# Row-column attention layer on one core: Yh kept in two f16 parts from the first half on, batch norm moved behind the product

## The reference

```
k = softmax over all 4096 pixels;  context = k v^T;  content_out = context^T q
Sx[n,i,x,y] = sum_d q[n,d,x,y] Px[x,i,d]           (Px: shifted rows of rel_rows)
Yh[n,e,x,y] = sum_i Sx[n,i,x,y] v[n,e,i,y]
Yh          = (Yh - mean_e) * rsqrt(var_e + 1e-5) * gamma_e + beta_e    (over n, x, y: all of Yh)
Sy[n,i,x,y] = sum_d q[n,d,x,y] Py[y,i,d]
rel[n,e,x,y] = sum_i Sy[n,i,x,y] Yh[n,e,x,i]
out = x + w_out (content_out + rel) + b_out
```

## Time and profile before

| | us |
|---|---|
| median of 3 runs | 3397.57 (3394.59 to 3403.66) |
| the profiled execution, its own time | 3392.93 |
| its span, first to last instruction | 3391.1 |
| mean granted TensorE clock | 0.922 of full |
| busy: PE, DVE, ACT, POOL | 2747.7, 2696.9, 1877.0, 1691.9 |
| second half's first instruction | about 2098 |

### The profile page before, as it was taken

One profiled execution on the slowest core, in us unless ns is written; L12 is line 12 of the kernel. 1 busy time (PEld: TensorE's weight loads), 2 busy tenths in 40 slices (PEclk: granted clock), 3 DMA queues, 4 the chain that ended last, 5 costly groups with the idle time before them and its releaser, 6 DMA issues. The chain is left out here.

```text
span 3391.1 us, 104576 instructions
## 1 busy us (share of the span) xinstructions
PE 2747.7 (81%) x42610; PEld 2165.2 (64%) x42610; DVE 2696.9 (80%) x3362; ACT 1877.0 (55%) x3268; POOL 1691.9 (50%) x856
## 2 busy tenths in 40 slices
PE   3897997997897997887897995578788797978788
PEld 2676786786786776776786784455565655555564
DVE  5798897898897898888888775787777869596875
ACT  2565664665665665665665663455554545455553
POOL 1344544544544544544544547675555646474651
PEclk9998998998998998998998997799899998989989
DMA  3133233233233233233231235465556565565653
GB/s 127 45 83 102 72 81 102 72 82 102 73 81 102 71 83 102 71 83 102 71 83 52 73 80 128 114 172 165 167 153 181 156 186 152 177 158 172 164 162 110
DMA packets 434977, 382.06 MB, mean 113 GB/s; under 512 B 299856, under 2 KB 366672, under 8 KB 432464
## 3 DMA queue, kind: packets, MB, share of 16 engines
q1 hardware_dynamic: 414992, 341.14, 36.8%
q10 hardware_dynamic: 19520, 34.15, 2.7%
HBM read 206.37 MB, written 168.82 MB: 111 GB/s over the span
## 5 line engine op out<-in xcount | busy, mean ns | idle before, releaser
L700 POOL TENSOR_TENSOR acc<-acc,yst 128x512 f32<-128x512 f32 x248 | 404.9, 1633 | 1013.7 <-DVE yst L635 1013.5
L360 PE MATMUL bank<-w_hi,x_hi 128*128 128x256 f16 x2048 | 572.8, 280 | 59.5 <-POOL x_lo L684 22.0
L1140 POOL TENSOR_TENSOR y_f<-y_f,y_mul 128x1024 f32<-128x1024 f32 x126 | 337.7, 2680 | 495.2 <-DMA y_f<-y_scratch 493.9
L1086 DVE TENSOR_TENSOR yb_lo<-y_f,yb_hi 64x1024 f16<-64x1024 f32 x256 | 522.9, 2043 | 77.2 <-ACT yb_hi L989 75.5
L360 PE MATMUL bank<-w_lo,x_hi 128*128 128x256 f16 x2048 | 565.4, 276 | 0.0
L360 PE MATMUL bank<-w_hi,x_lo 128*128 128x256 f16 x2048 | 565.1, 276 | 0.0
L935 PE MATMUL bank<-q,rc_both 128*64 128x64 f16 x4096 | 274.0, 242 | 162.2 <-DVE sy_lo L1098 127.3
L629 DVE SCALAR_TENSOR_TENSOR sx_lo<-bank,parity,sx_hi 128x512 f16<-128x512 f32 x512 | 355.3, 744 | 42.7 <-ACT sx_hi L485 42.7
L702 POOL TENSOR_TENSOR acc<-acc,ysq 128x512 f32<-128x512 f32 x248 | 386.2, 1557 | 0.0
L935 PEld LDWEIGHTS bank<-q,rc_both 128*64 128x64 f16 x4096 | 245.1, 133 | 189.8 <-DVE sy_lo L1098 134.0
L1143 POOL TENSOR_TENSOR y_f<-y_f,y_add 128x1024 f32<-128x1024 f32 x126 | 354.5, 2814 | 9.9
(11 more groups left out here) (146 smaller groups left out, 9605.7 us busy)
## 6 DMA issues: line engine op xcount, KB each, us to landing
y_scratch<-yst SPq DMA_DIRECT2D x512, 128.0 KB, 2.4
q<-q_scratch SPq DMA_DIRECT2D x256, 256.0 KB, 4.5
y_f<-y_scratch SPq DMA_DIRECT2D x256, 256.0 KB, 4.1
x_f<-x SPq DMA_DIRECT2D x16, 2048.0 KB, 11.3
q_scratch<-q_hi SPq DMA_DIRECT2D x64, 512.0 KB, 5.6
q_scratch<-q_lo SPq DMA_DIRECT2D x64, 512.0 KB, 7.2
x_res<-x SPq DMA_DIRECT2D x128, 256.0 KB, 3.9
out<-x_res ACTq DMA_DIRECT2D x128, 256.0 KB, 3.8
```

Source lines behind the costliest of these rows:

```text
L360: mm = pe.matmul(outs, lhs[a], rhs[m], start=first and n == 0, stop=last and n == 2, **kw)
L700: pool.tensor_tensor(acc[:, 0, :], acc[:, 0, :], yst[:, i % YST, :], ALU.add).then_inc(sums, 1)
L1086: o = dve.tensor_tensor(yb_lo[own, s, h, :], y_f[own, c, :, :], yb_hi[own, s, h, :], ALU.subtract)
L1140: pool.tensor_tensor(yy, yy, y_mul[:, :].unsqueeze(1).to_broadcast([P, XY, DK]), ALU.mult).then_inc(y_norm, 1)
```

## The change

In the first half ACT writes the f16 high part of 2^-8 Yh into `yst` (a new operation, line 497 of the changed kernel) ahead of the square, and waits for the store of the buffer; DVE writes the rest beside it instead of the copy. A row of `yst` is then 8 x (high, rest) x 64 f16, as many bytes as before, and is stored so. POOL's sum takes both parts, 1024 elements, and the squares 512; in the tail DVE and POOL change sides.

In the second half the y parts are loaded straight into the diagonal blocks of `yb_hi` and `yb_lo`: four transfers a piece, one a part and head, each of 64 partitions x 16 runs of 64 f16 (128 bytes). No normalisation and no split remain. The scale is put on the ro bank's rows by one column `y_col` while DVE adds the content part (`o_f`), and the shift is a matmul of `add_rows` with the sums of Sy over i. So there are two new kinds, ss (2 a unit: 16 matmuls of 512 columns with 32-column weights, split by ACT and DVE) and co (8 a unit: the eight context matmuls and one of 512 columns for the shift, copied by ACT to `content`); ro keeps 24 matmuls. `o_hi` is made by ACT from `o_f`, `o_lo` by DVE one ro later. There are six banks, a co bank is freed with its ro. y loads of unit t+1 are issued behind ro 1, 3, 5, 7 of unit t, ahead of the q piece of t+2, and sy of the next pair stand two ro earlier.

```diff
-SY_BEFORE = (0, 0, 0, 0, 1, 3, 5, 8)
+SY_BEFORE = (0, 0, 1, 3, 4, 6, 8, 8)
...
+                        if i == RO - 1:
+                            order += [("ss", hp + 1, j) for j in range(SS)]
-                    order.append(("ro", hp, i))
+                    order += [("co", hp, i), ("ro", hp, i)]
...
-                            act.activation(ysq[:, i % YSQ, :], src, ACT.Square).then_inc(hi_done, 1)
+                            act.activation(yst[:, i % YST, :, 0, :], src.rearrange("p (y e) -> p y e", e=DK),
+                                           ACT.Copy, scale=Y_SCALE)
+                            act.activation(ysq[:, i % YSQ, :], src, ACT.Square, scale=Y_SCALE).then_inc(hi_done, 1)
...
-                            dve.tensor_copy(yst[:, i % YST, :], src).then_inc(freed, 1)
+                            dve.scalar_tensor_tensor(yst[:, i % YST, :, 1, :], src.rearrange("p (y e) -> p y e", e=DK),
+                                                     Y_SCALE, yst[:, i % YST, :, 0, :],
+                                                     ALU.mult, ALU.subtract).then_inc(freed, 1)
...
-                    pool.tensor_tensor(acc[:, 0, :], acc[:, 0, :], yst[:, i % YST, :], ALU.add).then_inc(sums, 1)
+                    both = acc[:, 0:2, :].rearrange("p k n -> p (k n)")
+                    pool.tensor_tensor(both, both, yst[:, i % YST, :, :, :].rearrange("p y l e -> p (y l e)"),
+                                       ALU.add).then_inc(sums, 1)
...
                 def load_y(b, hp, c):
-                    for h in range(2):
-                        sp.dma_start(y_f[h * 64:h * 64 + 64, c, :, :].rearrange("p x e -> p (x e)"),
...
+                    for part, tile in enumerate((yb_hi, yb_lo)):
+                        for h in range(2):
+                            sp.dma_start(tile[h * 64:h * 64 + 64, c * XY:(c + 1) * XY, h, :],
+                                         y_dram[b * HP + hp].rearrange("g y h x l e -> h l (g y) x e")
+                                         [h, part, :, c * XY:(c + 1) * XY, :]).then_inc(y_in[c], 16)
...
                                 sp.wait_ge(filled, at2(b, ("ro", hp, i)) + 1)
-                                load_q(b, hp + 2, c)
-                                sp.wait_ge(yb_lo_done, (b * HP + (hp + 1)) * YC + (c + 1))
-                                load_y(b, hp + 2, c)
+                                load_y(b, hp + 1, i // 2)
+                                if more:
+                                    load_q(b, hp + 2, i // 2)
...
+                            mm = pe.matmul(bank[:, r, :], add_rows[own, :, :].rearrange("p h e -> p (h e)"),
+                                           s_rows[own, hp % 2, i // 4, :],
+                                           start=False, stop=True, skip_group_check=True)
...
                         elif kind == "ro":
-                            act.activation(o_hi[:, hp, i * BANK:(i + 1) * BANK], src, ACT.Copy).then_inc(hi_done, 1)
+                            act.wait_ge(freed, evacuated2(b, ("ro", hp, i)))
+                            act.activation(o_hi[:, hp, i * BANK:(i + 1) * BANK], o_f[:, i % 2, :],
+                                           ACT.Copy).then_inc(hi_done, 1)
...
+                            dve.scalar_tensor_tensor(o_f[:, i % 2, :], src, y_col[:, 0:1],
+                                                     content[:, i % 2, :], ALU.mult, ALU.add).then_inc(freed, 2)
+                            if last is not None:
+                                dve.wait_ge(hi_done, at2(b, ("ro", last[1], last[2])) + 1)
+                                split_output(*last)
```

332 lines of the change are left out of this document (182 added, 150 removed).

## The result

| kernel | median (runs' range) | profiled span | first ro's context starts | from there to the end |
|---|---|---|---|---|
| before | 3396.1 us (3389.8 to 3403.7) | 3391.1 us | 2159.5 us | 1231.6 us |
| changed | 3573.3 us (3569.2 to 3580.7) | 3574.7 us | 2265.4 us | 1309.3 us |

The change makes the kernel 5.2% slower: ratio 1.0523, 95% interval 1.0494 to 1.0553. The forecast was 3379 us, faster by 19, and its range ended at 3470. (In the text VectorE is the rows' DVE, ScalarE ACT, SyncE SP.) Of the 183.6 us between the two profiled spans, 105.9 lie ahead of the first ro and 77.7 behind it. The last stores of q in the first half begin to issue at 2064.6 us before and at 2189.0 now: by that mark the first half is 124.4 us longer, and the start of the second 18.5 us shorter.

A forecast was written before the change was run, and what follows sets the result against it. The prediction took DVE to bound the long part of an image, without pr, and PE the part with pr. Its terms, -62 - 16 - 19 + 78 = -19 us on 3397.6, gave 3379 us, range 3275 to 3470.

The forecast's parts named there:

- The sign: Whole kernel: faster by more than about 10 us had chance 0.49, slower by more 0.37, within that 0.14.
- The first half: Stretch with q and yh: POOL's longer sums and ACT's added instruction cost 2.5 us for 31 units, +78 us.
- Rival C: First half: POOL's adds cost in proportion to their length, +71 us on the forecast, 3450 us; chance 0.12.
- The start: Start of the second half: first ro at about 2141, some 15 us after POOL's power, -19 us.
- A unit without pr: Second half: a unit takes 25.7 us, with a wait for late q, instead of 28.3; -62 us in 24 units.
- after four y transfers at 0.58 us each: Last q piece of a unit: its second transfer starts to issue at 2.9 us, arriving 7.5 us after ro 7.
- The part with pr: Second half: PE's work grows by 2.6 us, idle shrinks, 68 becomes about 66; -16 us for eight images.
- Into the pr part it doesn't reach: Second half: the wait for q spares this part, as two pr stand ahead of each of the first four ro.
- The 128-byte packets: Second half's y loads: 12 ns a packet, y 12.3 us and q 9.1 us a unit, within the 25.7.
- Rival B: Second half: 128-byte packets decide, the gain gone at about 15 ns each; 3427 us, up to 3465; chance 0.2.
- The chain: Second half: o_f, o_hi and content need some 21 us a unit, just below PE's 22, so no bound.
- Rival A: Second half: q comes in time, a unit without pr takes 22 us, 3290 us in all; chance 0.25.

The follow-up runs named there:

- high_sum: In the changed kernel, POOL's running sum of Yh adds only the high f16 part in all units but each image's last; 3467.1 us, ratio 1.0216.
- high_nosq: On top of high_sum, ScalarE's square is left out and POOL adds constant ones in its place; 3425.3 us, ratio 1.0093.
- no_y: In the changed kernel, y is loaded for the first unit alone and never again; 3415.4 us, ratio 1.0069.
- all_four: Changed kernel with q issued ahead of y, next unit's sy later, y in 256-byte packets, and the sum edit of high_sum; 3347.9 us, ratio 0.9858.
- early7: all_four with the next unit's sy ahead of ro 3 to 6 in place of ro 4 to 7; 3337.0 us, ratio 0.9847.

## Why the prediction was wrong, by its steps

The forecast was -19 us, the profiled spans say +183.6. Of the 203 us between them 46 lie in the first half, 156 behind the first ro, and none in the start. The sign was wrong too; the prediction gave it 0.37.

**The first half** was forecast at +78 us and measured at +124.4. The step that failed is the path: the +78 are POOL's sums ending later and ScalarE waiting for them, and only POOL loses time, "POOL loses 0.8 to 1.0 us to each of DVE's 1.7 us operations". POOL's own loss was right. Its 1024-element addition takes 2.12 us at the least and 3.12 at the most, a spread of 1.0 us, as with the 512-element one. That agrees with the rule in "SBUF — State Buffer" of the Trainium skill (Who interferes with whom) as the prediction used it. Rival C's proportional loss did not come, though its sign, a first half longer by over 110 us, did. The durations (minimum, median, maximum) of the 512-element addition before and of the longer one after it are these:

```profile
L700 POOL TENSOR_TENSOR acc<-acc,yst x248: 1262/1290/2266, 144.0 to 2066.2; 128x512 f32<-128x512 f32 x124
```

```profile
L710 POOL TENSOR_TENSOR acc<-acc,yst x248: 2122/2157/3120, 142.0 to 2191.5; 128x1024 f32<-128x1024 f32 x124
```

But VectorE is held up too, and the prediction put that at nothing. VectorE was busy for 1668.6 of 2002 us there, so there was little room for it. Groups of unchanged work grew by 50.6 + 20.8 + 18.0 us, VectorE's busy time by 114.4, and high_sum takes nearly all of that back and with it 98.3 us of S. ScalarE's waits for POOL's sums, the forecast's path, grew by 15.7 us only (48.5 to 64.2). ScalarE's instruction was priced at 0.48 us at two places of a unit, about 1 us; 31 units of that are 30 us, and high_nosq gives 46, of which some 16 may be VectorE's busy time.

**The start**, forecast -19 us, measured -18.5: the mechanism was right, POOL's work on the four pieces is gone from the path, but the number was luck. The power on POOL,

```profile
L1212 POOL TENSOR_TENSOR var<-var,minus_half x1: 10539/10539/10539, 2246.4 to 2246.4; 128x64 f32<-128x64 f32 x1
```

ends at 2256.9 us, and the first ro's context starts 8.5 us later, not some 15. But the power started 57.4 us after the last q stores of the first half began to issue, against 50.9 before: 6.5 us that the forecast put at nothing. PE's statistics matmul waits 29.0 us for POOL's zeroing of the y weights there, 23.7 before.

**A unit without pr** was forecast at 25.7 us against 28.3, -62 us in all. By the same cut, the 87.1 us between two images' pr became 102.4, three units' worth, and the seven such stretches grew by 72 us. The mechanism was right, the late landing of q, three times an image. Its size failed at the step "after four y transfers at 0.58 us each". PE filled ro 7 at 2618.4 us, SyncE was busy with the piece before it until 2619.0, and from its first y issue to the start of the second q issue are 2625.1 - 2619.1 = 6.0 us, not 2.9, as two of the four y transfers take 1.6 to 1.7 us to issue. The landing took 4.3 us (forecast 4.5). So q came 11.1 us after the ro in place of 7.5, and PE, ready after 3.5 us (forecast 3.2), waited 7.6 in place of 4.3. This is the shortest of the image's three waits, and the mean of all 25 is 8.1 us. From q's arrival to the next ro 7 PE took 20.3 us (2629.5 to 2649.8), not 18.2, and the next q came at 2661.8: a unit of 32.3 us. Behind the wait the low clock adds 1.3 us that the forecast lacks (ro 0.58, context 0.39, shift 0.21, two sy 0.16, each against its next row of the chain or, for sy, the pair of 2.02 us at full clock).

**The part with pr** was forecast at -16 us for eight images, "68 becomes about 66". By the forecast's own cut the image has 65.3 us before and 64.9 now, and the eight stretches together are 6 us shorter: the sign was right, the size 10 us off. PE's added work was priced too low by one term. In the whole image PE's busy time grew by 13.6 us (123.5 to 137.1), where four units at 2.6 us make 10.4. The shift's matmul takes 0.32 us in the chain, not the 0.22 of a 512-column matmul in a row of its kind, which is 3.2 us for 32 of them. The sums were priced right, sixteen matmuls in 0.98 us (0.9 forecast):

```profile
2567.11 0.98 PE bank L975 x16
```

"Into the pr part it doesn't reach" held as well: the third wait for q ends at 2528.7, ahead of the first pr at 2536.3. In the windows cut at ScalarE's marks it falls into the stretch with pr, and is most of what that stretch lost against no_y.

**The 128-byte packets** were priced at 12 ns and took 12.8 where y is loaded alone; what one costs among the loads of q is not shown. The estimate of 9.8 ns from "DMA: Bandwidth & Descriptors" of the Trainium skill (Why small descriptors are slow) was further off. Rival B, with a price above 15 ns, did not come in at its price, nor its sign, a DMA share near 1 in the units without pr (0.77). Its total, 3427 to 3465, was nearer than mine for another reason: y in small transfers blocked the queue that issues it.

**The chain** `o_f`, `o_hi`, content is not the bound, as forecast: units of 23 to 27 us ran in all_four and early7 with the same chain (only the sy stand elsewhere). Rival A, q in time, gave 22 us a unit and 3290 us in all. The order in early7 comes near to that in the second half (48.5 us for two units) and not in the first.

## What to carry to other kernels

When a transfer becomes several smaller ones on one queue, price the issue and not the transfer alone, with the queue full, and put first in each piece what is needed first. When an engine gets a longer instruction on SBUF, look for what it does to the other engine's instructions, above all where that other engine is the bound. Compare a stretch before and after by the same work of the same engine: marks of another engine shifted a wait for q into a stretch that had not grown. And check a forecast that came true by its terms; two of the start's were off by 6.5 us each.
